# Two-layer transformer on one core: the output's high part ahead of the key's middle part in ScalarE's order, layer 2

## The reference

```python
# layer 1
x = x + _attention(_tc_rmsnorm(x, t, g1w, g1b, b1w, b1b), Wq, Wk, Wv, Wo)
return x + _swiglu(_tc_rmsnorm(x, t, g2w, g2b, b2w, b2b), gate_w, hid_w, out_w)   # hidden size 1024
...
# layer 2
q, k, v = (proj(Wq), proj(Wk), proj(Wv))
scores = jnp.einsum('bhsd,bhtd->bhst', q, k) * scale
scores = jnp.where(mask[None, None, :, :], -jnp.inf, scores)
out = jnp.einsum('bhst,bhtd->bhsd', jax.nn.softmax(scores, axis=-1), v)
out = out.transpose(0, 2, 1, 3).reshape(B, S, E) @ Wo.T
# then an RMS norm, a scale and a shift from the conditioning
...
# whole
x = x + layer_1(x); x = x + layer_2(x)
```

## Time and profile before

| | us |
|---|---|
| median of 3 runs | 1013.13 (1011.05 to 1015.7) |
| the profiled execution, whole | 1008.46 |
| its span, first to last instruction | 1006.6 |
| TensorE matmuls busy | 909.2 (90%) |
| weight loads busy | 780.6 (78%) |
| VectorE busy | 570.3 (57%) |
| ScalarE busy | 547.5 (54%) |
| GpSimd busy | 415.2 (41%) |
| DMA transfers, share of 16 engines | 39.8% |

### The profile page before, as it was taken

One profiled execution on the slowest core, in us unless ns is written; L12 is line 12 of the kernel. 1 busy time (PEld: TensorE's weight loads), 2 busy tenths in 40 slices (PEclk: granted clock), 3 DMA queues, 4 the chain that ended last, 5 costly groups with the idle time before them and its releaser, 6 DMA issues.

```text
span 1006.6 us, 24326 instructions
## 1 busy us (share of the span) xinstructions
PE 909.2 (90%) x8188; PEld 780.6 (78%) x8188; DVE 570.3 (57%) x1104; ACT 547.5 (54%) x1130; POOL 415.2 (41%) x633
## 2 busy tenths in 40 slices
PE   3578899999999999999999999999999789888874
PEld 3456698898888988988889889889887677777653
DVE  3366556557555565575565756545455455555541
ACT  2246556546455565464554665554556566666652
POOL 5223344443443444434334344344444454444522
PEclk9779999999999999999999999999999999999997
DMA  6555423322332233223322242232437576576611
GB/s 204 110 106 122 91 64 75 75 65 59 66 86 42 63 73 73 63 58 68 84 42 63 69 91 65 65 76 66 94 74 167 119 160 147 142 166 144 157 36 34
DMA packets 83070, 91.29 MB, mean 91 GB/s; under 512 B 7776, under 2 KB 70016, under 8 KB 83008
## 3 DMA queue, kind: packets, MB, share of 16 engines
q1 hardware_dynamic: 83008, 90.50, 39.8%
HBM read 60.30 MB, written 29.36 MB: 89 GB/s over the span
## 4 chain that ended last, share of the span: by engine, by line
PE 73%; issue 8%; DVE 7%; ACT 5%; POOL 3%; DMA 1%; SPq 1%; POOLq 0%; DVEq 0%; ACTq 0%
PE work L525 11%; PE work L527 11%; PE work L526 11%; PE pvps L622 8%; PE s2ps L606 7%; PE s1ps L583 5%; PE work L710 4%; PE acc L525 3%; PE acc L526 2%; PE acc L527 2%; PE work L656 2%; PE s1ps L568 2%; PE work L718 1%; DVE rest L919 1%; DVE th L959 1%
## 5 line engine op out<-in xcount | busy, mean ns | idle before, releaser
L1055 ACT ACTIVATE E<-s2ps 128x512 f32<-128x512 f32 x384 | 214.1, 596 | 184.2 <-PE s2ps L606 110.8
L882 DVE TENSOR_REDUCE nmax<-s1ps 128x2 f32<-128x512 f32 x256 | 163.9, 682 | 32.1 <-PE s1ps L583 31.9
L525 PE MATMUL work<-xch,Gh 128*128 128x256 f32 x512 | 154.5, 302 | 0.0
L959 DVE SCALAR_TENSOR_TENSOR th<-th,work 128x256 f32<-128x256 f32 x128 | 53.8, 420 | 168.7 <-ACT th L1073 168.7
L1328 POOL TENSOR_TENSOR hl<-hf,hh 128x256 fp32r<-128x256 f32 x128 | 94.9, 742 | 131.0 <-PE acc L527 77.3
L526 PE MATMUL work<-xcl,Gh 128*128 128x256 f32 x512 | 147.1, 287 | 0.0
L527 PE MATMUL work<-xch,Gl 128*128 128x256 f32 x512 | 146.9, 287 | 0.0
L606 PE MATMUL s2ps<-stack 100*128 100x256 bf16 x768 | 127.7, 275 | 2.1 <-DMA stack<-rows 2.0
L875 DVE TENSOR_REDUCE nmax<-s1ps 128x4 f32<-128x512 f32 x128 | 85.6, 685 | 36.5 <-PE s1ps L568 36.4
L525 PEld LDWEIGHTS work<-xch,Gh 128*128 128x128 f32 x512 | 99.3, 194 | 8.2 <-issue 6.6
L622 PE MATMUL pvps<-E,vaug 128*32 128x256 f32 x1536 | 97.5, 387 | 6.3 <-ACT E L1055 4.0
(11 more groups left out here) (131 smaller groups left out, 2149.1 us busy)
## 6 DMA issues: line engine op xcount, KB each, us to landing
stack<-scr SPq DMA_DIRECT2D x64, 384.0 KB, 4.6
stack<-scr SPq DMA_DIRECT2D x64, 256.0 KB, 5.2
scr<-qp SPq DMA_DIRECT2D x64, 192.0 KB, 2.3
scr<-kp SPq DMA_DIRECT2D x64, 192.0 KB, 2.3
stack<-scr SPq DMA_DIRECT2D x64, 128.0 KB, 5.6
X<-xT SPq DMA_DIRECT2D x16, 256.0 KB, 4.5
yT<-crm SPq DMA_DIRECT2D x16, 256.0 KB, 5.2
stack<-rows SPq DMA_DIRECT2D x196, 4.0 KB
```

The costliest lines, as they stand in the source:

```text
L525: mm(out, lh, rh, start=first, stop=False, skip_group_check=True)
L882: v.tensor_reduce(nmax[:, g // 4, qh, 2 * (g % 4):2 * (g % 4) + 2], s1ps[u % 2][:, :].rearrange("p (h t) -> p h t", h=2), AX_X, ALU.max, n ...
L959: v.scalar_tensor_tensor(th[:, i % 2, :], th[:, i % 2, :], 1.0, bank[:, 0:T], ALU.add, ALU.mult).then_inc(silu_ready, 1)
L1055: a.activation(E[:, exp_slot(st.L["B2"], st.full, g, kh), :], s2ps[g % 2 if short else u % 2][:, :], ACT.Exp, scale=SCORE_SCALE).then_inc( ...
```

## The change

In the steps whose stage A works on an item of layer 2 (steps 14 to 29), ScalarE's K middle is no longer the last entry of slot 1. It stands in slot 2, behind the copy `oh` and the exponentials of that slot, and ahead of the closing norm's two affine operations. For layer 1, K middle stands at the end of slot 2, as before. No other engine's list changes.

```diff
--- before.py
+++ after.py
@@ -1144,6 +1144,8 @@
                         bank, _ = opened(st, "K")
                         after(act, k_written, 32 * st.n(2))
                         a.copy(kp[:, 2, :, :].rearrange("p c t -> p (c t)"), bank[:, :]).then_inc(k_high, 1)
+                    if g == 2 and L["A"] == 1:
+                        middle(st, "K", kp, k_mid)
                     if g == 2 and L["R"] is not None:
                         n = st.n(-2)
                         b, k = st.bank("bcR")
@@ -1185,7 +1187,7 @@
                         a.copy(Wh[:, m, :, :], nrm[:, :, :]).then_inc(swap_hi, 1)
                     if g == q_slot(L):
                         middle(st, "Q", qp, q_mid)
-                    if g == q_slot(L, 1):
+                    if g == 2 and L["A"] == 0:
                         middle(st, "K", kp, k_mid)
                     if g == 5 and st.s0 in RAW_SPLIT:
                         raw_high(RAW_SPLIT[st.s0])
```

## The result

The changed kernel takes 1040.16 us (median of 4 runs, 1037.99 to 1044.08), the kernel before 1013.45 on the same occasions: a ratio of 1.0268, 95% interval 1.0226 to 1.031, or 26.7 us slower. The forecast was 1024.6 with a range up to 1030. The sign was right; the 11.5 us forecast are less than half of what came.

A forecast was written before the change was run, and what follows sets the result against it. It took TensorE's own work as most of the chain, with a loop through the DMA queue setting the later steps. 7.3 + 4.2 = 11.5 us on the 1013.13 median gave 1024.6, range 1016 to 1030.

The forecast's parts named there:

- Part 1: Steps 14 to 17: late K middle delays GpSimd's K low and `hl`, so TensorE's down projection waits; +7.3 us.
- Rival B: Delay in steps 14 to 17 is absorbed, only the later loop grows: +4.2 us, so 1017.3; chance 0.07.
- Part 2: Steps 19 to 29: `oh` starts earlier, so TensorE's output projection waits less for `ol`, 1.0 us earlier a step.
- its caveat: The 1.0 us TensorE gains does not come off; it becomes a wait at `s1ps` and `s2ps` of slot 0.
- Part 3: Steps 19 to 30: late K middle lengthens the loop through SP's DMA queue by 0.45 a step; +4.2 us in sum.
- The slack of 0.1: Room in the DMA-queue loop before slot 0's scores, about 0.1 us a step, taken off the 0.55 delay.
- Rival C: New stalls also cost clock: one fall in each of four steps, 4 us more, so 1028.6; chance 0.08.
- Rival A: Not slower: the queue is not the bound and slot 0's scores come earlier with TensorE, so 1009.4; chance 0.10.

The follow-up runs named there:

- e1: K middle moved in steps 14 to 17 alone, against the kernel before: 1022.73 us, ratio 1.0096.
- e2: K middle moved in steps 18 to 29 alone, against the kernel before: 1030.11 us, ratio 1.0187.
- e4: Changed kernel, with SP's reads of the stack's second half issued only once the shift rows landed, from step 18: 1020.1 us; changed kernel 1040.16.
- e3: Kernel before, with K middle right behind `oh` and ahead of the exponentials from step 18, so K is not late: 1018.85 us, ratio 1.0059.
- e6: e3 plus SP's second-half reads held until the shift rows landed, from step 18: 1007.68 us, ratio 0.9933 to the kernel before.
- e7: Changed kernel, with matmuls of constants filling TensorE's waits at slot 0 in steps 19 to 29: 1030.15 us; changed kernel 1040.16.
- e5: Kernel before, with SP's second-half reads held until the shift rows landed, from step 18: 1010.86 us, ratio 0.9973.

## Why the prediction was right and wrong

**Part 1 was right.** The mechanism, its place and its size (7.3 forecast, 7.2 measured in the waits) held. About 1.5 us more were lost in step 15 by the clock, which part 1 did not count. Rival B, which had it absorbed, is refuted by e1.

**Part 2 was right, with its caveat.** TensorE got the output projection 1.0 us earlier, and it came to nothing in the sum.

**Part 3 was mis-sized: +4.2 forecast, about 17 measured (e2).** The step that failed is "The change makes this loop 0.55 longer, less a slack of 0.1 on average: +0.45 a step", with its upper bound of 0.55 a step: it took everything in the loop but the late K as fixed, and the clock as whole. Measured at full clock it was +0.9 a step, and the falls of the clock came on top. The late K is real. The transposes end and K middle starts:

```profile
819.70 0.60 PE L670 MATMUL work<-ident,on 128*128 128x128 f32 x4
...
821.32 0.61 ACT L1102 CAST kp<-rest 128x512 bf16<-128x512 f32 x1
```

1.02 apart, where the earlier trace rows have 0.56. The store, too, comes 8.01 us behind K high (827.48 and 819.47) instead of 7.55 (809.56 and 802.01). But I took the way from the store to the rows' completion as a fixed 0.67. It was so short because the rows used to come late, with the second half's reads later still. With `oh` early, SP issues both earlier, and the completion of the rows goes to 1.0 to 1.5 behind the store. That is shown by e4, which removes it alone, and by e3, which has it alone. The step that starts at 819.47 takes 18.32 instead of 17.42, three stretches of it end to end: 0.46 more from K high to the store, 0.44 more from the store to the scores (6.81 instead of 6.37), and the same 3.50 from there to the next K high. The prediction's list of what stands behind K middle ends with the shift rows; the second half's reads, which SP issues right behind them, are not in it.

The slack of 0.1 was wrong as well. It was read from a step without a wait, which tells when the scores started and not when the rows were there. With the reads held back, the loop takes 16.9 with K on time (e6), and 17.4, as in the kernel before, with K late (e4). So the room was about 0.5 a step, and the late K alone used it up without costing anything against the kernel before. The reads behind the rows alone took it and a little more (most steps of e3 take 17.6 to 17.8 at full clock); both together gave 17.9 to 18.7, and with that the falls of the clock.

**The clock was a rival with 0.08, and mostly in the wrong place.** Rival C put it in steps 14 to 17 and gave it 4 us, 1 in each step; there it fell in step 15 alone, for about 1.5 us. It cost 9 to 10 us (e7) in steps 19 to 29, where the new waits of slot 0 add up to about 2 to 3 us in a row with one matmul group between. I had priced a fall at 1 us from the earlier trace rows; between two of the windows above it is 1.6 (20.0 against 18.4). The Trainium skill (TensorE: Matmul & The Clock Gate, Part 1) says that a throttled clock is the default and that activity releases it. The trace agrees as far as e7 goes: with constants multiplied in the waits the granted clock is 1.00. Which of several like steps loses its clock (857 to 876 kept it, 896 to 916 did not) is not settled by any run here.

**Rival A** (the queue has slack, 1009.4) fell with the trace of after. The page that the prediction cites for it, in the Trainium skill (Perfetto Trace Analysis, Optimization Strategies), speaks of engines that block the critical path, and in the changed kernel the shorter wait for `ol` only lengthened the waits of slot 0 for the queue. Once the queue is out of the way the earlier `oh` pays: a step of 16.9 in e6 against 17.4 in e5, which differ in nothing else.

Not settled: by what the second half's reads delay the rows. The Trainium skill (DMA: Bandwidth & Descriptors, Queues, rings and completion order) says that a DMA engine takes descriptors in order, and that a completion is held back by the writes ahead of it, but also that a later transfer may finish its write before an earlier one. It does not say what later reads cost the small writes ahead of them; here the scores start 0.5 to 0.7 behind the store's landing without these reads and 1.0 to 1.5 with them. Whether it is shared bandwidth or the order of the writes was not tried.

## What to carry to other kernels

When a wait shrinks, ask what the engine behind it will now issue earlier, and into which queue: a large transfer issued early can delay the small urgent one just ahead of it. Two paths of nearly the same length show one wait only; the path without waits has to be measured by its own period before the other is cut. A short new stall of TensorE is to be priced with the clock it may cost, and an entry of an in-order list with all that stands behind it on the next engine.

## What the runs showed of the hardware

The scores that wait for transfers of 4 KB started 0.5 to 0.7 us behind the landing of the 256 KB store ahead of them when nothing followed the small ones (most steps of e4 and e6), and 1.0 to 1.5 behind it when 768 KB of reads were issued right after them (the changed kernel, ten steps); holding those reads back gained 20 us. Fifteen useless matmuls in each of 11 steps made the changed kernel 10 us faster, with a granted clock of 1.00 instead of 0.95 (e7).
